# First head-mixing stage of a twelve-stage network on one core: sums over products moved to TensorE, one VectorE operand read from PSUM, fewer GpSimd products

## What is computed

```python
b, s, dm = x.shape            # 4, 1024, 128
h, hd = (H, dm // H)          # 16, 8
Q = (x @ Wq.T).reshape(b, s, h, hd)
K = (x @ Wk.T).reshape(b, s, h, hd)
V = (x @ Wv.T).reshape(b, s, h, hd)
scores = jnp.einsum('bshd,bstd->bsht', Q, K) / math.sqrt(hd)
attn = jax.nn.softmax(scores, axis=-1)
out = jnp.einsum('bsht,bstd->bshd', attn, V).reshape(b, s, dm)
return out @ Wfc.T
...
x = x + _L0_attn_ref(_layernorm(x, axis=-1), L0_attn_Wq, L0_attn_Wk, L0_attn_Wv, L0_attn_Wfc)
```

## Time and profile before

| what | value |
|---|---|
| median of the runs | 3564.93 us |
| profiled execution | 3569.27 us |
| its span, first to last instruction | 3567.5 us |
| mean granted TensorE clock, share of full speed | 0.805 |
| HBM traffic over the span | 33 GB/s |
| PE busy, share of the span | 2273.6 us, 64% |
| DVE busy | 2385.7 us, 67% |
| ACT busy | 1323.2 us, 37% |
| POOL busy | 1031.8 us, 29% |

### The profile page before, as it was taken

One profiled execution on the slowest core, in us unless ns is written; L12 is line 12 of the kernel. 1 busy time (PEld: TensorE's weight loads), 2 busy tenths in 40 slices (PEclk: granted clock), 3 DMA queues, 4 the chain that ended last, 5 costly groups with the idle time before them and its releaser, 6 DMA issues. The chain is left out here.

```text
span 3567.5 us, 42404 instructions
## 1 busy us (share of the span) xinstructions
PE 2273.6 (64%) x12704; PEld 1343.6 (38%) x12704; DVE 2385.7 (67%) x5649; ACT 1323.2 (37%) x2721; POOL 1031.8 (29%) x917
## 2 busy tenths in 40 slices
PE   3494212213958588888888886769366594577774
PEld 2494111113954212222222223558245593322223
DVE  4456987875564888888778753445655456577776
ACT  0262100001632347767667672136111362122221
POOL 4542656563430000000000001544233342122220
PEclk9996555555979779989889888779676796688997
DMA  4122000000220500000000000012200122000000
GB/s 130 46 65 70 0 12 6 8 10 24 64 81 1 210 24 17 17 15 17 15 15 17 14 1 7 30 47 63 83 18 19 41 65 63 21 0 0 0 0 24
DMA packets 118253, 121.31 MB, mean 34 GB/s; under 512 B 21936, under 2 KB 101648, under 8 KB 117264
## 3 DMA queue, kind: packets, MB, share of 16 engines
q1 hardware_dynamic: 98720, 72.79, 7.0%
q0 software_dynamic: 17840, 40.55, 3.1%
q10 hardware_dynamic: 1472, 5.26, 0.4%
HBM read 67.14 MB, written 50.99 MB: 33 GB/s over the span
## 5 line engine op out<-in xcount | busy, mean ns | idle before, releaser
L1659 DVE TENSOR_REDUCE attn_mx<-bank 128x1 f32<-128x512 f32 x1024 | 653.3, 684 | 150.2 <-PE bank L1464 146.8
L1577 ACT ACTIVATE attn_pT<-bank 128x512 f32<-128x512 f32 x1024 | 561.0, 599 | 261.4 <-PE bank L1478 255.5
L1464 PE MATMUL bank<-attn_K,attn_Q 48*128 48x512 bf16 x1024 | 386.3, 423 | 145.1 <-DVE attn_mx L1659 129.7
L1478 PE MATMUL bank<-attn_Q,attn_K 51*128 51x512 bf16 x1024 | 373.0, 413 | 5.3 <-ACT attn_pT L1577 4.7
L1633 POOL TENSOR_TENSOR attn_m_rem<-attn_m_rem,attn_m_parts 8x128 f32<-8x128 f32 x128 | 53.3, 416 | 873.4 <-ACT attn_m_parts L1590 873.4
L1491 PE MATMUL bank<-attn_pT,attn_vb 128*32 128x512 f32 x2048 | 298.3, 657 | 1.0 <-ACT attn_pT L1577 1.0
L1464 PEld LDWEIGHTS bank<-attn_K,attn_Q 48*128 48x128 bf16 x1024 | 88.5, 94 | 534.8 <-DVE attn_mx L1659 437.4
L426 ACT ACTIVATE xnT<-bank 128x512 f32<-128x512 f32 x64 | 38.2, 597 | 410.4 <-PE bank L381 410.4
L2290 POOL TENSOR_TENSOR mix_rS<-mix_rT,mix_S 128x512 f32<-128x512 f32 x64 | 81.5, 1277 | 303.0 <-ACT mix_gT L2270 203.3
L952 POOL TENSOR_TENSOR mix_pool_pv<-mix_prob,mix_qkv 128x2048 f32<-128x2048 f32 x24 | 131.9, 5496 | 25.0 <-DVE mix_mixed L1032 18.1
L381 PE MATMUL bank<-ident,mix_norm_xn 128*128 128x128 f32 x64 | 15.6, 391 | 174.8 <-DVE mix_norm_xn L227 174.8
(11 more groups left out here) (594 smaller groups left out, 5863.2 us busy)
## 6 DMA issues: line engine op xcount, KB each, us to landing
attn_q_parts<-attn_rope_q_parts SPq DMA_DIRECT2D x48, 128.0 KB
attn_k_parts<-attn_rope_k_parts SPq DMA_DIRECT2D x48, 128.0 KB
attn_Q<-attn_q_parts SPq DMA_DIRECT2D x64, 96.0 KB
attn_K<-attn_k_parts SPq DMA_DIRECT2D x64, 96.0 KB
ffn0a_x_ring<-xs_rows SPq DMA_DIRECT2D x72, 64.5 KB
ffn0b_x_ring<-xs_rows SPq DMA_DIRECT2D x72, 64.5 KB
ffn2a_x_ring<-xs_rows SPq DMA_DIRECT2D x72, 64.5 KB
ffn2b_x_ring<-xs_rows SPq DMA_DIRECT2D x72, 64.5 KB
```

What stands on the lines that cost most here:

```text
L1464: nc.tensor.matmul(a_bank[hf][:], slot(net.Q, h, 0, KROWS)[:, qt * P:(qt + 1) * P], slot(net.K, h, 0, KROWS)[:, hf * CH:(hf + 1) * CH], st ...
L1478: nc.tensor.matmul(s_bank[hf][:], slot(net.K, h, 0, KROWS + MROWS)[:, kt * P:(kt + 1) * P], slot(net.Q, h, 0, KROWS + MROWS)[:, hf * CH:(h ...
L1577: nc.scalar.activation(pT[:, kt % RING, hf * CH:(hf + 1) * CH], s_bank[hf][:], ACT.Exp, scale=HD ** -0.5).then_inc(exp_ready, 1)
L1659: nc.vector.tensor_reduce(mx[:, h % 2, qt, hf:hf + 1], a_bank[hf][:], AX.X, ALU.max).then_inc(a_used, 1)
```

## The change

`L0_wqkv` grows to 512 columns: q with the element of the head outermost, v as before, k with the element outermost, v with the element outermost. A tile n is now a step of the loop by itself, the loop runs from -2, and the products of tile n+2, the maxima of n+1 and the values of n are worked in step n. Tiles 0 and 1 of each chunk are "summed".

- Scores, all tiles: VectorE multiplies q, read from the PSUM bank where the matmul left it, by k in SBUF (`times_keys`). TensorE adds the eight 256-column slices of the product, as eight matmuls with the identity accumulating in PSUM (`sum_scores`). VectorE takes maximum and difference straight from PSUM.
- Values, tiles 0 and 1: GpSimd multiplies, TensorE adds sixteen 128-column slices (`sum_values`).
- Values, tiles 2 and 3: ScalarE writes the exponentials into PSUM, VectorE multiplies them by v in SBUF and sums (`times_values` of VectorE).
- GpSimd makes 2 products of a chunk in place of 5. `scatter` and `place` come one chunk later than before, `rank` too. The copy `xa` of the input is gone; products, tables and `mixed` have two buffers, `kv` eight.

The diff without the removed lines (the functions as they were are printed above):

```diff
-    n.L0_wqkv = sb("L0_wqkv", [P, 3 * D])
+    n.L0_wqkv = sb("L0_wqkv", [P, 4 * D])
...
+        HH, KV, SUMMED = H * H, 8, (0, 1)
+        kv = part.sb("kv", [P, KV, 2 * D])
+        prod_qk = part.sb("prod_qk", [P, 2, HD * HH])
+        prod_pv, own_pv = part.sb("prod_pv", [P, 2, HD * HH]), part.sb("own_pv", [P, HD * HH])
+        logit, prob = part.sb("logit", [P, 2, HH]), part.sb("prob", [P, 2, HH])
+        top, den, rden = part.sb("top", [P, 2, H]), part.sb("den", [P, 2, H]), part.sb("rden", [P, 2, H])
+        mixed_tiles, mixT = part.sb("mixed", [P, 2, CH]), part.sb("mixT", [P, CH])
+        qkv_bank, s_bank, m_bank, y_bank = net.bank[0:2], net.bank[2:4], net.bank[4:6], net.bank[6]
...
+        def is_summed(n):
+            return n % TPC in SUMMED
+        def summed_before(n):
+            return n // TPC * len(SUMMED) + min(n % TPC, len(SUMMED))
+        def prob_of(n):
+            if is_summed(n):
+                return prob[:, summed_before(n) % 2, :]
+            return m_bank[n % 2][:, HH:2 * HH]
+            def qkv(n):
+                need(pe, qk_done, n - 1)
+                need(pe, kv_kept, n - 1)
+                nc.tensor.matmul(qkv_bank[n % 2][:], src[:, n * P:(n + 1) * P], net.L0_wqkv[:],
+                                 start=True, stop=True).then_inc(qkv_ready, 1)
+            def sum_scores(n):
+                pe.wait_ge(qk_done, n + 1)
+                need(pe, logit_ready, n - 1)
+                for d in range(HD):
+                    ins = nc.tensor.matmul(s_bank[n % 2][:, 0:HH], net.ident[:], prod_qk[:, n % 2, d * HH:(d + 1) * HH],
+                                           start=(d == 0), stop=(d == HD - 1))
+                ins.then_inc(s_ready, 1)
+            def sum_values(n):
+                a = summed_before(n)
+                pe.wait_ge(pv_done, a + 1)
+                need(pe, mixed, n - 1)
+                for t in range(H):
+                    ins = nc.tensor.matmul(m_bank[n % 2][:, 0:D], net.ident[:], prod_pv[:, a % 2, t * D:(t + 1) * D],
+                                           start=(t == 0), stop=(t == H - 1))
+                ins.then_inc(sum_ready, 1)
...
+            qkv(0)
+            for n in range(-2, NTT):
+                c, i = divmod(n, TPC)
+                if n > 0 and i == 0:
+                    turn_mixed(c - 1)
+                if i == 2 and c > 0:
+                    pe.wait_ge(y_added, c)
+                    norm.turn(pe, c - 1)
+                if n + 3 < NTT:
+                    qkv(n + 3)
+                if n + 2 < NTT:
+                    sum_scores(n + 2)
+                if n > 0 and i == 0:
                     project(c - 1)
+                    if c > 1:
+                        norm.rank(pe, c - 2)
+                if n >= 0 and is_summed(n):
+                    sum_values(n)
+                if i == 2 and c > 0:
                     norm.logits(pe, c - 1, router.rw)
+            c = NCH - 1
...
+            keep(0)
+            for n in range(-2, NTT):
+                c, i = divmod(n, TPC)
+                if n > 0 and i == 0:
                     keep_mix(c - 1)
+                if n + 3 < NTT:
+                    keep(n + 3)
+                if 0 <= n + 1 < NTT:
+                    exp(n + 1)
+                if i == 2 and c > 0:
                     norm.keep(act, c - 1)
...
+            def times_values(n):
+                a = summed_before(n)
+                pool.wait_ge(exp_ready, n + 1)
+                need(pool, sum_ready, a - 1)
+                shape = [P, H, H, HD]
+                p = grid(prob_of(n), H).rearrange("p h t -> p t h")
+                v = grid(kv[:, n % KV, 0:D], HD)
+                nc.gpsimd.tensor_tensor(prod_pv[:, a % 2, :].rearrange("p (t h d) -> p t h d", h=H, d=HD),
+                                        bcast(p.rearrange("p t (h z) -> p t h z", z=1), shape),
+                                        bcast(v.rearrange("p (t z) d -> p t z d", z=1), shape), ALU.mult).then_inc(pv_done, 1)
+            for c in range(NCH):
+                for i in SUMMED:
+                    times_values(c * TPC + i)
+                if c > 0:
                     norm.rstd_pow(pool, c - 1)
+                if c > 1:
+                    norm.scatter(pool, c - 2)
+                if c > 0:
                     norm.grow(pool, c - 1)
+            norm.scatter(pool, NCH - 2)
+            norm.all_pool(pool, NCH - 1)
+            norm.all_scattered(pool)
...
+            def times_keys(n):
+                dve.wait_ge(kv_kept, n + 1)
+                need(dve, s_ready, n - 1)
+                at = D if is_summed(n) else 0
+                shape = [P, HD, H, H]
+                q, k = grid(qkv_bank[n % 2][:, 0:D], H), grid(kv[:, n % KV, at:at + D], H)
+                nc.vector.tensor_tensor(prod_qk[:, n % 2, :].rearrange("p (d h t) -> p d h t", h=H, t=H),
+                                        bcast(q.rearrange("p d (h z) -> p d h z", z=1), shape),
+                                        bcast(k.rearrange("p (d z) t -> p d z t", z=1), shape), ALU.mult).then_inc(qk_done, 1)
+            def below_top(n):
+                s = grid(s_bank[n % 2][:, 0:HH], H)
+                dve.wait_ge(s_ready, n + 1)
+                need(dve, logit_ready, n - 1)
...
+                need(dve, exp_ready, n - 1)
+                nc.vector.tensor_tensor(grid(logit[:, n % 2, :], H), s, bcast(grid(top[:, n % 2, :], 1), [P, H, H]),
+                                        ALU.subtract).then_inc(logit_ready, 1)
...
+            def scale(n):
+                c, i = divmod(n, TPC)
+                need(dve, mix_turned, c - 1)
+                nc.vector.tensor_tensor(grid(mixed_tiles[:, c % 2, i * P:(i + 1) * P], HD), grid(m_bank[n % 2][:, 0:D], HD),
+                                        bcast(grid(rden[:, n % 2, :], 1), [P, H, HD]), ALU.mult).then_inc(mixed, 1)
+            def times_values(n):
+                shape = [P, H, HD, H]
+                p, v = grid(prob_of(n), H), grid(kv[:, n % KV, D:2 * D], H)
+                chain.then(nc.vector.tensor_tensor(own_pv[:].rearrange("p (h d t) -> p h d t", d=HD, t=H),
+                                                   bcast(p.rearrange("p (h z) t -> p h z t", z=1), shape),
+                                                   bcast(v.rearrange("p (z d) t -> p z d t", z=1), shape), ALU.mult))
+                chain.wait()
+                chain.then(nc.vector.tensor_reduce(m_bank[n % 2][:, 0:D], own_pv[:].rearrange("p (m t) -> p m t", t=H),
                                                    AX.X, ALU.add))
...
+            for n in range(-2, NTT):
+                c, i = divmod(n, TPC)
+                if n + 2 < NTT:
+                    times_keys(n + 2)
+                if n > 0 and is_summed(n - 1):
+                    dve.wait_ge(sum_ready, summed_before(n - 1) + 1)
+                    scale(n - 1)
+                if 0 <= n + 1 < NTT:
+                    below_top(n + 1)
+                if n >= 0:
+                    share(n)
+                    if not is_summed(n):
+                        times_values(n)
+                        scale(n)
+                if c > 1 and i == 0:
+                    norm.place(dve, c - 2)
+                if c > 0 and i == 0:
                     add(c - 1)
                     norm.stats(dve, c - 1)
+                if c > 0 and i == 1:
                     norm.apply(dve, c - 1)
+                if c > 0 and i == 3:
                     norm.pick(dve, c - 1, router.rb)
                     norm.weigh(dve, c - 1)
+            norm.place(dve, NCH - 2)
+            add(NCH - 1)
+            norm.all_dve(dve, NCH - 1, router.rb)
+            norm.table(dve)
...
-    a["L0_wqkv"] = np.concatenate([g["L0_attn_Wq"].T, g["L0_attn_Wk"].T, g["L0_attn_Wv"].T], axis=1)
+    by_dim = np.arange(D).reshape(H, HD).T.reshape(-1)
+    wq, wk, wv = (g["L0_attn_W" + k].T for k in "qkv")
+    a["L0_wqkv"] = np.concatenate([wq[:, by_dim], wv, wk[:, by_dim], wv[:, by_dim]], axis=1)
```

More of the change, by code:

```diff
@@ L893, in _ @@
+            c = NCH - 1
+            turn_mixed(c)
+            norm.rank(pe, c - 1)
+            project(c)
+            pe.wait_ge(y_added, c + 1)
+            norm.all_pe(pe, c, router.rw)
+            norm.count(pe)
         @block.scalar
         def _(act):
-            def keep(c, i):
-                act.wait_ge(qkv_ready, c * TPC + i + 1)
-                need(act, mixed, (c - 1) * TPC + i + 1)
-                nc.scalar.activation(qkv[:, i, :], net.bank[i][:, 0:3 * D], ACT.Copy).then_inc(qkv_kept, 1)
@@ L906, in keep_mix, with exp @@
+            def exp(n):
+                if is_summed(n):
+                    need(act, pv_done, summed_before(n) - 1)
+                need(act, mixed, n - 1)
+                act.wait_ge(logit_ready, n + 1)
+                nc.scalar.activation(prob_of(n), logit[:, n % 2, :], ACT.Exp, scale=HD ** -0.5).then_inc(exp_ready, 1)
             def keep_mix(c):
@@ L1016, in gather @@
[L1016 to L1028 removed]
+            STEPS = 3
```

(12 more changed lines are left out.)

193 lines of the change are left out of this document (31 added, 162 removed).

## The result

The changed kernel takes 3452.26 us (median of 4 runs, 3438.88 to 3474.8) against 3559.47 (4 runs); the ratio is 0.9706 with a 95% interval of 0.9644 to 0.9768. The forecast was 3477, the range 3420 to 3520. The profiled execution took 3474.8 us over a span of 3473.0; it is the longest of the four.

A forecast was written before the change was run, and what follows sets the result against it. VectorE was taken as nearest the bound, partly held by GpSimd's products. Nine chain items gave 50.6 us a steady chunk against 62.0, the stage 388.0 against 475.8, 87.8 less: 3477 us, range 3420 to 3520.

The forecast's parts named there:

- step 2: Chunk's second step on VectorE: scale, maxima and difference, share, product and sum, scale; 6.65 us.
- step 3: Chunk's third step on VectorE: as the second, with one product of 2.25 more and without the first scale; 8.65 us.
- item 2: TensorE behind `times_keys` of tile 2: scores 6.3, hand-over 0.1, projection 1.3, `rank` 2.3; 10.0 us in all.
- The charge for the clock: TensorE sum after a pause: 5.7 us slow, the remaining fifth fast, 6.3 in all; sums right behind it 3.4.
- Item 9: Rest of `weigh`, SBUF operands alone, waits until GpSimd's product ends: 5.35 + 0.5 = 5.85 us.
- Item 5: TensorE's scores of tile 3 and values of tile 1, 6.85, plus 1.0 for hand-over and low clock: 7.85 us.
- It stands 4.3 us above the median: Step from profiled execution to median: the profiled 3481.5 us, taken as 4.3 above the median, gives 3477.
- q repeated from PSUM: Rival: `times_keys` reads the repeated q slowly, 3.83 us each, 34 us in all: 3511; chance 0.15.
- The low clock: Rival: TensorE stays at 1.2 GHz and its chain takes 61.9 us a chunk: 3579; chance 0.07.
- VectorE's long products: Rival: products by k and by v take 5.4 us each, 118 us in all: 3595; chance 0.07.
- The faster rival's: Rival: `weigh` slips ahead of GpSimd's product, -5.2 us, 3446; TensorE at full clock from the start, 3424; chance 0.17.
- VectorE's freedom from GpSimd: Claim: VectorE instructions with only SBUF tensors wait for GpSimd's running product, 10.2 us a round; one PSUM operand avoids it.

The follow-up runs named there:

- idle matmuls: The grow first kernel with 12 unused identity matmuls behind `rank` from chunk 2 on: 3379.3 us, ratio 0.9500; also tried as the 80 matmuls.
- The repeat: The changed kernel measured once more without any edit: 3439.6 us, ratio 0.9676.
- 80 matmuls: The changed kernel with 80 unused identity matmuls before the sum of scores of tile 2 in chunks 2 to 7: 3492.1 us, ratio 0.9818.
- regrouped: Changed kernel, projection and `rank` before tile 2's score sum; GpSimd's queue: `rstd_pow`, tile 1 product, `scatter`, next chunk's tile 0 product, `grow`: 3409.4 us, ratio 0.9576.
- both SBUF changes: The changed kernel with q and exponentials in SBUF, and GpSimd's next product waiting until `weigh` has ended: 3411.5 us, ratio 0.9603.
- no hold: The changed kernel with one wait added, so GpSimd starts its next product only when `weigh` has ended: 3404.9 us, ratio 0.9583.
- all in SBUF: The changed kernel with q and the exponentials of tiles 2 and 3 in SBUF for VectorE's long products: 3426.5 us, ratio 0.9676.
- `rank` early: The changed kernel with the projection and `rank` ahead of the sum of scores of tile 2 on TensorE: 3412.7 us, ratio 0.9608.
- grow first: The regrouped kernel with `scatter` moved behind `grow` to the end of GpSimd's queue: 3378.9 us, ratio 0.9514.
- scatter late: The changed kernel with `scatter` moved behind `grow` in GpSimd's queue, ahead of the next product: 3447.9 us, ratio 0.9710.

## Why the prediction was right, and where it was off

The steps, beside the round from 538.97 to 588.10:

| item | forecast | measured | from rows |
|---|---|---|---|
| 1 `times_keys` 2 | 2.25 | 2.3 | L998 |
| 2 scores, projection, `rank` | 10.0 | 7.4 | 541.26 to 548.66 |
| 3 `place`, `add`, `stats` | 3.2 | 3.2 | to 551.86 |
| 4 `times_keys` 3 | 2.25 | 2.3 | to 554.15 |
| 5 scores 3, values 1 | 7.85 | 7.4 + 3.0 gap | to 564.51 |
| 6 step 2 | 6.65 | 6.5 | to 571.00 |
| 7 step 3 | 8.65 | 8.5 | to 579.48 |
| 8 `pick`, `grow` | 3.9 | 4.0 | to 583.44 |
| 9 rest of `weigh` | 5.85 | 4.7 | to 588.10 |

The sum is 49.1 against 50.6; the next round is 50.2, with 8.5 in item 2. The direction and the chain were right: nine items in this order, one wait on `rank`, one hold in `weigh`, and six of the nine within 0.2 us. The stage came out 96.9 us shorter against 87.8: 4.9 of the 9.1 are the five steady rounds, 5.0 chunk 1, 1.0 chunk 0, and the last chunk takes 1.8 back.

- *Item 2 was sized too high by 1.5 to 2.6 us.* The charge for the clock was right in kind (0.50 at the start of the sum; the idle matmuls show it) and near in size (5.2 to 6.7 for 6.3; 5.4 in the round above, which is 0.9 of its 2.6). The rest stood behind it: projection and `rank` take 1.05 and 1.2 us at the full clock, which the sum ahead of them has brought back, where I had 1.3 and the 2.3 of the row of before.
- *Item 9 was 1.2 us too high* for GpSimd's product: 4.05 us, not the 5.35 of L952. Its order (source head outermost, eight elements inside) is another than the two of before. The mechanism stood, and the run without the hold took 3.8 us off.
- *Item 5 missed the gap of 3.0 us*; its sum by itself was right within 0.5. Without the gap the item would have been 0.5 too high. These three errors partly cancel, which is luck: without the gap the round is 46.6, four us under the forecast.
- *Chunk 1* took 42.2 us, not 47.2: no gap, and its first sum at the full clock (3.7). Chunk 0 took 43.6 for 44.6; the last 45.0 for 43.2, the gap again.
- *From the stage to the kernel.* "It stands 4.3 us above the median" was carried over to the changed kernel. There the profiled execution stood 22.5 above the median, mostly through the attention stage. The profiled execution itself was forecast at 3481.5 and took 3474.8; most of the 25 us between 3477 and 3452 (18.2) are this step, not the stage. The repeat bears it out: its profiled execution was 33.0 us shorter than the first and its attention stage 30.5.

The rivals. *q repeated from PSUM* fell: 2283 ns in the mean of 32, 2292 at most. The rule of the Trainium skill ("Vector Engine (DVE) Microarchitecture Reference", section 5.2), as I read it, gave an estimated 3.7 us; the measurement decides, and this source, which repeats each word sixteen times, did not behave as one that hops. *The low clock* fell: 0.81 over the stage, 0.85 in the round. *VectorE's long products* stayed at 2.2 to 2.3. *The faster rival's* two terms are both real, but neither came by itself: `weigh` did not slip ahead of the product in any chunk of 1 to 6 (L269 4.02; it does so, for 3.8 us, when made to), and the clock was lost before the first sum in each chunk from 2 on.

What I had for the reason of the gain needs one correction. The prediction gave VectorE's freedom from GpSimd to the operand in PSUM. That freedom is real (2.23 us against 4.05 in chunk 0), but with everything in SBUF the steady rounds are as short. In this order of work VectorE is free because its long products and GpSimd's hardly meet.

## What stays open

The gap of 3.0 to 4.6 us before `scale` of tile 1. It appears in the changed kernel, its repeat, the one with 80 matmuls and the regrouped one, in each chunk that scatters, and in the one with both SBUF changes in the last chunk alone (2.3 us). It is absent in the other seven, of which the one without GpSimd's product has no such sum. VectorE and ScalarE, which both wait for TensorE there, go on within 0.1 us of each other, and where the gap is, it ends 1.4 to 1.7 us after the last scatter issue has, whenever the sum ended. That points to the landing of the scatter. But in three kernels without the gap (no hold, all in SBUF, `rank` early) `scatter` lies beside the same sum, at the same distance in the first.

The rival is the chip, and it fits better than any order: all four kernels profiled on chip 15 have the gap in some chunk, none of the seven on chips 7 and 11 has it. A second thing goes with it. Counted in the packed traces, the five with a gap hold 27,202 to 27,437 updates of semaphores over the whole execution, all others, the kernel before included, 31,999 to 32,084; most of the missing ones are landings of DMAs, and they are missing from the first 350 us on, ahead of the stage. So something was different before any edited instruction ran. The kernel with both SBUF changes, which has the records missing and no gap in chunks 2 to 6, says that this alone isn't enough. Running the regrouped kernel and the one with grow first on one chip would settle it; no run does. Whether the last 8 us, those of the idle matmuls, are a gain of the whole kernel is open as well.

## What to carry to other kernels

An engine that shares its access with another is best given its long instructions while the other waits for something else or has already started its own; one wait did more here (3.8 us of a round, 6.9 with the gap) than taking GpSimd's work away (2.0, 5.0 with the gap), and a new order of two queues did most (6.4 us on one chip). Look for a hold in short instructions (a 4-column operation of 4.02 us), and after each move ask which short ones the product meets next. Judge a change to one stage by that stage's rows, since a stage it does not touch may differ by 30 us between two executions. And run the kernels that are to be compared on one chip: a 3 us gap in each chunk can't be laid to an edit when the chip changed with it.

## What the runs showed of the hardware that was not expected

- GpSimd's product of 2048 columns takes 4.05 us with v's eight elements innermost and the probability repeated over them, 5.35 in the order of before.
- The exclusion between VectorE and GpSimd works both ways and for whole instructions: 6.1 us for a product of GpSimd that starts 0.14 us behind a VectorE product of 2.29 with both operands in SBUF. Two products of GpSimd in a row leave no room between them: the instruction of `place` that waits took up to 7.5 us (scatter late).
- Not every VectorE instruction on SBUF is held: reductions and reciprocals that began inside a product kept 2.23 and 0.25 us, eighteen of eighteen. GpSimd's DMA issues hold no instruction of `weigh` (0.17 us beside them).
- An operand that repeats each element sixteen times is read from PSUM as fast as one from SBUF: 2283 ns for 2048 columns, where L943 of the kernel before took 2280.
- Two engines that waited for TensorE went on together, 2.3 to 4.6 us late, in five profiles, which are also the ones with some 4,700 semaphore updates missing. The cause is open.
